# Attention over 32 patterns, two layer norms and a small FFN: two of four chunks of the output product in three passes of rounded parts, probabilities in five sets of blocks

## The reference

```python
queries = query @ Wq + bq                     # query: 16 x 1024 x 512, 16 heads of 32
keys    = key_param @ Wk + bk                 # 32 patterns
values  = keys @ Wv + bv
A   = sparsemax(scale * scores(queries, keys))
x   = layernorm(query + (A @ values) @ Wo + bo)
s   = x @ Win + bin_                          # 64 units
g   = einsum(relu(s[..., None] * W1 + b1), W2) + b2
out = layernorm(x + g @ Wout + bout)
```

## Time and profile before

| | |
|---|---|
| median of 3 runs | 1311.17 us (1311.08 to 1311.61) |
| the profiled execution | 1313.41 us, its span 1311.6 us |
| mean granted TensorE clock over the span | 0.983 |
| PE busy | 1248.0 us, 95% |
| DVE, ACT, POOL busy | 1133.2 us (86%), 1068.2 us (81%), 676.5 us (52%) |
| bytes moved by DMA | 258.35 MB, mean 197 GB/s |

### The profile page before, as it was taken

How to read it: one execution, slowest core, us unless ns; L and a number is a source line. 1 busy time by engine, 2 the same in 40 slices (tenths; PEclk the granted TensorE clock), 3 DMA queues, 4 the chain that set the end, 5 groups by cost and what they waited for, 6 DMA issues and landing times. The chain is left out here.

```text
span 1311.6 us, 25223 instructions
## 1 busy us (share of the span) xinstructions
PE 1248.0 (95%) x5848; PEld 853.4 (65%) x5848; DVE 1133.2 (86%) x4538; ACT 1068.2 (81%) x2285; POOL 676.5 (52%) x1634
## 2 busy tenths in 40 slices
PE   8973899999999999999999999999999999989995
PEld 5642566676766767676776767677676767655552
DVE  3986899899999999999999999999999999966776
ACT  3661865779898888989898888989898888987776
POOL 1431333346555555655565555656555555665654
PEclk9995999999999999999999999999999999999998
DMA  6480785655656556565656656565655656468874
GB/s 203 131 215 17 199 246 192 191 185 171 218 184 216 198 197 206 190 217 182 220 188 208 203 191 214 185 220 183 213 196 199 211 186 216 162 227 281 280 233 104
DMA packets 92181, 258.35 MB, mean 197 GB/s; under 512 B 16067, under 2 KB 16067, under 8 KB 75622
## 3 DMA queue, kind: packets, MB, share of 16 engines
q1 hardware_dynamic: 91862, 256.26, 60.0%
q10 hardware_dynamic: 144, 0.26, 0.1%
HBM read 206.13 MB, written 50.33 MB: 196 GB/s over the span
## 5 line engine op out<-in xcount | busy, mean ns | idle before, releaser
L856 PE MATMUL bank<-G_sb,pT 128*128 128x512 f32 x1024 | 462.5, 594 | 2.8 <-DMA G_sb<-G_of_heads 2.1
L856 PEld LDWEIGHTS bank<-G_sb,pT 128*128 128x128 f32 x1024 | 185.2, 191 | 188.6 <-issue 184.3
L1426 DVE SCALAR_TENSOR_TENSOR acc<-hinge,w2c,acc 128x512 f32<-128x512 f32 x210 | 157.1, 748 | 81.7 <-ACT hinge L1019 80.2
L541 POOL TENSOR_TENSOR shift_sq<-sum,per_row_sq 128x1 f32<-128x1 f32 x244 | 95.2, 390 | 252.4 <-DVE y_sb L1269 250.5
L1376 DVE MAX8 top<-bank 128x8 f32<-128x32 f32 x2048 | 211.8, 178 | 0.0
L749 PE MATMUL bank<-A_hi,xT_hi 128*128 128x512 f32 x512 | 203.3, 397 | 0.0
L751 PE MATMUL bank<-A_hi,xT_lo 128*128 128x512 f32 x512 | 202.7, 396 | 0.0
L750 PE MATMUL bank<-A_lo,xT_hi 128*128 128x512 f32 x512 | 202.6, 396 | 0.0
L1019 ACT ACTIVATE hinge<-s_sb,b1c,w1c 128x512 f32<-128x512 f32 x240 | 192.8, 806 | 0.0
L1075 ACT CAST xT_hi<-bank 128x512 fp32r<-128x512 f32 x127 | 74.1, 584 | 134.8 <-PE bank L751 134.8
L989 ACT ACTIVATE unread<-y_sb,shift_sq 128x512 bf16<-128x512 f32 x244 | 174.5, 715 | 7.7 <-POOL minus_mean L543 7.5
(11 more groups left out here) (164 smaller groups left out, 2461.7 us busy)
## 6 DMA issues: line engine op xcount, KB each, us to landing
G_sb<-G_of_heads SPq DMA_DIRECT2D x128, 1024.0 KB, 5.5
x_sb<-in_L_attn_query_dram SPq DMA_DIRECT2D x128, 256.0 KB, 4.7
y_sb<-in_L_attn_query_dram SPq DMA_DIRECT2D x256, 128.0 KB, 5.4
out_dram<-o_sb SPq DMA_DIRECT2D x230, 128.0 KB, 4.7
G_of_heads<-y_sb SPq DMA_DIRECT2D x64, 256.0 KB, 4.0
out_dram<-y_sb SPq DMA_DIRECT2D x11, 256.0 KB, 3.3
y_sb<-in_L_attn_Wk_dram SPq DMA_DIRECT2D x1, 1024.0 KB, 5.9
y_sb<-in_L_attn_Wq_dram SPq DMA_DIRECT2D x1, 1024.0 KB, 8.1
```

Source lines behind the costliest of these rows:

```text
L541: nc.gpsimd.tensor_tensor(shift_sq[:, par:par + 1], total[:, par:par + 1], per_row_sq[:], ALU.mult).then_inc(s_mean, 1)
L856: mm = nc.tensor.matmul(o_ps[i % 2][:], pT[:, bass.ds(pair_place(turn, i) + (i % H * C + c) * P, P)], G_sb[:, i % GR, c, :], start=(c == 0 ...
L1426: nc.vector.scalar_tensor_tensor(acc[:], hinge[:, k % HR, :], w2c[:, k:k + 1], acc[:], ALU.mult, ALU.add).then_inc(s_acc, 1)
```

## The change

Chunks 1 and 3 of the output product (IN_PARTS) are kept as two fp32r tensors, a rounded high part and the rest, for G and for the probabilities, and multiplied in three passes. Chunks 0 and 2 (RAW) stay plain fp32. A head of G then has six pieces of 256 KB. ACT writes each piece of an IN_PARTS unit twice (as it is and rounded), POOL subtracts the two, and SP stores the high parts and the low parts separately, the low ones a slot later in its list. POOL makes the parts of the probabilities one slot ahead of the product. G gets a ring of 3 instead of 2 and is loaded one slot earlier. `pT` shrinks from two full turns (8 sets of four blocks) to five sets of four blocks whose places rotate from turn to turn; ACT now writes a batch as one contiguous block, after the products that freed its place.

```diff
-LAG_G = 22
+LAG_G = 21
+LAG_PART = 22
-        GR, STAGES = 2, 2
+        GR, SETS = 3, 5
+        IN_PARTS, SPREAD = (1, 3), 6
-        pT = sb("pT", [P, 2 * H * C * P])
+        pT = sb("pT", [P, SETS * C * HPC * P])
+        part_hi = sb("part_hi", [P, 2, len(IN_PARTS) * P], F32R)
+        part_lo = sb("part_lo", [P, 2, len(IN_PARTS) * P], F32R)
-        G_sb = sb("G_sb", [P, GR, C, D])
+        G_sb = sb("G_sb", [P, GR, SPREAD, D], F32R)
...
# SP, slot
-                for k in pieces(turn, j - 2):
...
+                for k in pieces(turn, j - 2)[HPC - 1:]:
                     heads, c, a = piece(k)
+                    if in_parts(k):
+                        sp.wait_ge(s_Ghi, parts_to(k))
+                        store_unit(heads, hi_col(c), STAGE_HI, s_Gst_hi)
+                    else:
+                        sp.wait_ge(s_Gev, k + 1)
+                        store_unit(heads, raw_col(c), STAGE_RAW, s_Gst_raw)
+                for k in pieces(turn, j - 3)[HPC - 1:]:
+                    heads, c, a = piece(k)
+                    if in_parts(k):
+                        sp.wait_ge(s_Glo, parts_to(k))
+                        store_unit(heads, lo_col(c), STAGE_LO, s_Gst_lo)
...
# POOL, slot: after the norms and the FFN's two ops, ahead of the means
+                if in_range(turn, j, LAG_PART):
+                    i = base + j - LAG_PART
+                    rows = p_blocks[:, parts_rows(i), i % HPC, :]
...
+                    nc.gpsimd.tensor_copy(part_hi[:, i % 2, :]..., rows).then_inc(s_phi, 1)
+                    pool.wait_ge(s_phi, i + 1)
+                    nc.gpsimd.tensor_tensor(part_lo[:, i % 2, :]..., rows, part_hi[:, i % 2, :]...,
+                                            ALU.subtract).then_inc(s_plo, 1)
...
# POOL, slot: at its end, after the folds
+                for k in [*pieces(turn, j - 2)[HPC // 2:], *pieces(turn, j - 1)[:HPC // 2]]:
+                    if in_parts(k):
+                        a = k % HPC
+                        pool.wait_ge(s_Ghi, parts_to(k))
+                        nc.gpsimd.tensor_tensor(y_sb[:, STAGE_LO + a, :].bitcast(F32R), y_sb[:, STAGE_LO + a, :],
+                                                y_sb[:, STAGE_HI + a, :], ALU.subtract).then_inc(s_Glo, 1)
...
# PE
+            def output_product(i):
+                o, G = o_ps[i % 2], G_sb[:, i % GR]
+                for c in RAW:
+                    nc.tensor.matmul(o[:], p_blocks[:, block_of(i, c), i % HPC, :], G[:, raw_col(c), :].bitcast(F32),
+                                     start=(c == RAW[0]), stop=False)
+                pe.wait_ge(s_plo, i + 1)
+                for n, c in enumerate(parts_of(i)):
+                    hi, lo = (part[:, i % 2, n * P:(n + 1) * P] for part in (part_hi, part_lo))
+                    nc.tensor.matmul(o[:], hi, G[:, hi_col(c), :], start=False, stop=False)
+                    nc.tensor.matmul(o[:], hi, G[:, lo_col(c), :], start=False, stop=False)
+                    mm = nc.tensor.matmul(o[:], lo, G[:, hi_col(c), :], start=False, stop=(n == len(IN_PARTS) - 1))
+                return mm
...
# ACT, probabilities
-                        act.wait_ge(s_o, base + (lead - lead % UNROLL) - 2 * UNROLL + h0 + HPC)
+                    if its_turn > (0 if c else 1):
+                        act.wait_ge(s_o, (its_turn - 1) * H + c * HPC)
...
# ACT, pieces
-                    if k % HPC == 0 and k >= HPC * STAGES:
-                        act.wait_ge(s_Gst[k // HPC % STAGES], 16 * HPC * (k // HPC // STAGES))
-                    nc.scalar.copy(y_sb[:, k % (HPC * STAGES), :], G_ps[k % HPC][:]).then_inc(s_Gev, 1)
+                    stored = 16 * HPC * (k // HPC // 2)
+                    if in_parts(k):
+                        if a == 0 and k >= 2 * HPC:
+                            act.wait_ge(s_Gst_hi, stored)
+                            act.wait_ge(s_Gst_lo, stored)
+                        nc.scalar.copy(y_sb[:, STAGE_LO + a, :], G_ps[a][:]).then_inc(s_Gev, 1)
+                        nc.scalar.copy(y_sb[:, STAGE_HI + a, :].bitcast(F32R), G_ps[a][:]).then_inc(s_Ghi, 1)
+                    else:
+                        if a == 0 and k >= 2 * HPC:
+                            act.wait_ge(s_Gst_raw, stored)
+                        nc.scalar.copy(y_sb[:, STAGE_RAW + a, :], G_ps[a][:]).then_inc(s_Gev, 1)
```

More of the change, by code:

```diff
@@ L353, in so_far, with block_of, parts_of, parts_rows @@
             return min(max(n, 0), TILES) if isinstance(n, int) else n
-        def pair_place(turn, i):
-            return (turn + i // UNROLL) % 2 * (H * C * P)
+        blocks, spare = [{(n, c): n * C + c for n in range(C) for c in range(C)}], list(range(C * C, C * C + C))
+        for _ in range(1, TILES // UNROLL):
+            old = blocks[-1]
+            blocks.append({(n, c): old[c - 1, n] if c else spare[n] for n in range(C) for c in range(C)})
+            spare = [old[C - 1, c] for c in range(C)]
+        p_blocks = pT[:].rearrange("p (b a n) -> p b a n", a=HPC, n=P)
+        def block_of(i, c):
+            return blocks[i // UNROLL][i % H // HPC, c]
+        def parts_of(i):
+            return sorted(IN_PARTS, key=lambda c: block_of(i, c))
+        RAW = [c for c in range(C) if c not in IN_PARTS]
+        def parts_rows(i):
+            first, last = (block_of(i, c) for c in parts_of(i))
+            return slice(first, last + 1, last - first)
+        def raw_col(c):
+            return RAW.index(c)
+        def hi_col(c):
+            return len(RAW) + 2 * IN_PARTS.index(c)
+        def lo_col(c):
+            return hi_col(c) + 1
+        STAGE_RAW, STAGE_LO, STAGE_HI = 0, HPC, 2 * HPC
         def turns_of(turn, j, lag, ring):
@@ L391, in piece, with in_parts, parts_to @@
             return k // (HPC * C), k // HPC % C, k % HPC
+        def in_parts(k):
+            return piece(k)[1] in IN_PARTS
+        def parts_to(k):
+            return sum(in_parts(n) for n in range(k + 1))
         def group_of(turn, i):
@@ L438, in _, with store_unit @@
             AHEAD = 2
+            def store_unit(heads, col, stage, s_stored):
+                for n in range(HPC):
+                    places = G_dram[HPC * heads + n].rearrange("(a s) n -> s a n", s=S)
+                    sp.dma_start(places[:, :, col * D:(col + 1) * D],
+                                 y_sb[n * S:(n + 1) * S, stage:stage + HPC, :]).then_inc(s_stored, 16)
             def slot(turn, j):
@@ L462, in slot @@
                         if h % HPC == 0:
[L463 to L467, removed]
+                            units = h // HPC + 1
+                            sp.wait_ge(s_Gst_raw, 16 * HPC * len(RAW) * units)
@@ L851, in slot @@
                         pe.wait_ge(s_Gev, PIECES)
[L852 removed]
+                    pe.wait_ge(s_G[(base + i) % GR], 16 * ((base + i) // GR + 1))
                     if not isinstance(turn, int) or base + i >= 2:
                         pe.wait_ge(s_r1, base + i - 1)
[L855 to L859, removed]
+                    output_product(base + i).then_inc(s_o, 1)
                 if in_range(turn, j, LAG_YT):
```

49 lines of the change are left out of this document (26 added, 23 removed).

## The result

The changed kernel takes **1377.24 us** (median of 4 runs, 1374.51 to 1378.37) where the kernel before took 1311.12 us beside it: a ratio of 1.0502, 95% interval 1.0484 to 1.052. The forecast was 1375 us. The profiled execution took 1377.7 us with a span of 1375.9 us, 64.3 us over the 1311.6 us of before.

What follows compares the result with a forecast made beforehand. PE was taken to bound the main loop at 9.20 us a slot. From the profiled 1313.4 us, -19 (main loop), +73 (making G) and +10 (late slots) gave 1377, less 2.2 for the median: 1375 us, range 1342 to 1412.

Steps and rivals of the forecast that it cites:

- Making G: Start, while G is made: new waits on stored low parts, extra copies and a low clock cost +73 us (56 to 90).
- The chain: Start: ACT waits through POOL's folds, two late subtractions and SP's store; two slots take 21.1 us, not 10.6.
- about +9.5: Start: us lost per stall in slot pairs with probabilities, below +10.5 elsewhere because some PE work gets done during the stall.
- the 11 us for the clock: Start: stalls idle PE, so five later products with A run at the low clock, 2.2 us each (ends 0 and 15).
- Main loop: Some 105 slots of output products: shorter PE work gains 19 us (ends -34 and +30).
- The saving on PE: Main loop: two plain chunks become six fp32r passes, 0.32 us a slot off PE, at most 33.6 us.
- I take a gain of 0.18 us, a little over half of PE's: Main loop: gain per slot, cut from 0.32 because POOL's new work might stretch DVE operations; 105 slots give -19 us.
- Rival 1: Main loop: DVE becomes the bound, gaining nothing or losing up to 0.29 us a slot; 1394 to 1424 us, chance 0.14.
- Late slots: Last stretch: loads of G grow from 1.05 to 1.57 MB, costing +10 us (ends -4 and +20).
- 330 GB/s at most: Late slots: DMA limit taken from 287 GB/s at 87% busy, making a slot 6.36 us against 5.46.
- the third buffer: Late slots: it brings part of one load forward, so +10 us was taken where the loads alone gave 12.6.
- one slot of four: Main loop: POOL is late from the FFN's two ops there, so ACT's squares come up to 1.5 us later.

## Why the prediction was right

**Making G, +82.1 for +73.** The mechanism was right. The chain that the prediction read from the lists alone is the one that runs: ScalarE's wait is released by the store, the store by the late subtractions, and each link taken out gives its time back. A wait of 9.5 to 10.7 us was forecast as 9 to 10. Its links measured 6.4 us for the store (6.3 taken) and 1.36 us a subtraction (1.05 taken, with 1.46 as the far end: the two-input operation writing fp32r is nearer to the fold's price per element than to L613's). The mis-sized term is "about +9.5" for pairs with probabilities and the 11 us for the clock with it. Pairs without probabilities lost 11.9 to 12.1 us (10.5 and 2.2 were taken), but two of the pairs with them lost 15.3 each. Little work of PE was done under the stall there: PE stands at the second half of the probabilities (L902, 43.1 us behind ScalarE's copies, 12.2 to 12.4 us in each of the three pairs), in order, and everything behind it comes after the restart, at the low clock (0.53 from 73 to 91 us). The third of these pairs, with no pieces of G behind it, lost 12.5 us. The runs without the stall lose both at once; how the 15.3 us divide between clock and order was not separated.

**Main loop, -32.6 for -19.** The saving on PE was right, 941.15 - 908.51 = 32.6 us, 0.317 a tile of 0.32. The step that failed is "I take a gain of 0.18 us, a little over half of PE's": GpSimd's new work stretches VectorE's operations by 0.02 us (`u_sb`) and 0.10 us (`twice`) a tile, not by a microsecond, and VectorE stays under TensorE's pace. The reason for caution was sound for another cause: the run with two passes finds the next wall at 8.765 us a tile, 0.055 us below, and the runs with more work or another order on GpSimd stand at 8.88 to 9.12. Rival 1 (VectorE becomes the bound) fell by that much.

**Late slots, +14.2 for +10.** Loads set the pace in this trace, as forecast: PE waits 11.8 us for them. But that 6.36 us was forecast and 6.35 measured is partly luck. The slot moved some 2.03 MB (319 GB/s x 6.35 us), not 2.10, and "330 GB/s at most", scaled up from 287 GB/s at 87%, is no limit: the same loads went at 338 and 348 GB/s in two other runs, with 5.94 and 5.78 us a slot. The relief that was hoped for from the third buffer did not come here. Not foreseen was the second wait under it: with short loads GpSimd's rounding ahead of the means costs 6.7 us (one run), which the prediction had put only at "one slot of four" in the main loop.

**The sum.** +9.1, -13.6 and +4.2 us of error cancel to -0.3. The total was better than its parts.

## What to carry to other kernels

When a stage of a buffer is reused, follow the release through every engine's list in order: here two operations put one slot later on GpSimd turned a free wait into 10 us, six times, and making them and their store a slot earlier took 60 us off. Weigh a larger operand against the stretch in which the DMA engines are already at 87%, as a gain in the main loop is given back there; but do not scale a rate up by the busy share to find the limit, as the same loads went at 319 to 348 GB/s. And when one engine's work is cut, measure the next wall by cutting more than the change does: it lay 0.055 us away.

## What was not expected of the hardware

The granted clock fell while TensorE was busy. In the run with idle passes it read 1.00 from 99.7 to 108 us, with 0.90 us of idle time in between, and then 0.50 for a stretch in which PE ran short passes and pieces of G without a gap (windows, columns as above):

```profile
99.70:106.00 6.30, 6.29 (x30) 5.17 (x28) 0.62 (x4) 0.33 (x1) 1.05 (x1) 1.00 0.86 208
106.00:108.00 2.00, 1.12 (x3) 0.39 (x3) 0.00 (x0) 2.00 (x5) 0.00 (x0) 1.00 0.00 1
...
110.00:120.00 10.00, 10.00 (x17) 4.68 (x17) 6.88 (x27) 4.66 (x12) 4.97 (x5) 0.50 0.55 133
120.00:123.00 3.00, 3.00 (x11) 2.42 (x10) 0.00 (x0) 0.00 (x0) 0.00 (x0) 0.50 0.98 206
123.00:125.00 2.00, 2.00 (x10) 1.48 (x8) 0.00 (x0) 0.00 (x0) 0.00 (x0) 0.94 0.79 208
```

It came back at 123 us, behind the first passes of the next product with A. Being busy, as the profile counts it, did not keep the clock up there. Whether the gap of 0.90 us or the kind of work brought it down, this run does not tell; behind a gap of 0.79 us at 93.8 us in the same run it stayed at 1.00.

And an engine's busy share said little of its room: GpSimd at 76% of the main loop (226.61 of 300) had no room for 1.1 us more in a slot of 8.82: the loop grew to 9.12, and ScalarE's wait for the means grew with it.
